# Attention and expert layer on one core: which probability chunks a DMA turns, and where the first expert's weight pieces are split

## The chip, the core and the metric

The kernel runs on one core of a Trainium2 chip. Five engines work side by side and wait for each other over semaphores: PE (TensorE, matrix products), DVE (VectorE), ACT (ScalarE), POOL (GpSimd) and SP (SyncE, which here only issues DMAs). The metric is the device time of one execution in microseconds (us), as the median of several runs.

## The reference

```python
xn = layernorm(x)                                  # x: 2 sequences x 2048 tokens x 256, float32
scores = (xn @ W_qk) @ xn.T / 16 + (kpos - qpos) * slope     # causal
s = softmax(scores) @ (xn @ W_v.T)
probs = softmax(xn @ Wr)                           # 8 experts, the best one per token
# each expert takes its first 512 tokens
ye = relu(xe @ W1[e]) @ W2[e] * p_tok              # W1: 256 x 1024, W2: 1024 x 256
out = x + s * silu(scatter(ye))
```

## The kernel before

Numbers in float32 are held as a high and a low half in float16, and each product is three matmuls (high x high, high x low, low x high). ACT writes the high half, DVE the low half, which is the number minus the high one.

The 4096 tokens are 32 tiles of 128 rows, 16 per sequence. Tile t of a sequence attends to the keys up to itself, in chunks of four blocks of 128 keys: `chunks(t)` is 1 for the first four tiles of a sequence, then 2, 3, and 4 for tiles 12 to 15 and 28 to 31. A tile goes through these steps, chunk by chunk:

- `score` on PE writes 128 x 512 scores into one of two banks of PSUM; DVE's `score` (L965) reads them, adds the bias and keeps the least value. A bank is free for the next but one chunk only then. PE works one tile ahead: in tile t it makes the scores of tile t + 1.
- `probs` on ACT takes the exponential, after the last chunk's least value (`rmin`).
- The chunk has to be turned, so that keys lie on partitions. There are two ways. PE's `turn` (L1409) makes four 128 x 128 transposes into PSUM, from which ACT (`high`, L1224) and DVE (`low`, L984) write the halves into `pT`. Or, where `by_dma(t, c)` holds, ACT and DVE write the halves of the rows into one of two buffers `p_rows`, and SP issues one transposing DMA into `pT` (`chunk_turn`, L522). ACT's `high` of such a chunk waits until the DMA of the next but one before it, in the same buffer, has landed.
- `values` on PE (L1420) multiplies the turned chunk with the values, 12 matmuls for four blocks, in tile t + 1; for a chunk turned by DMA it waits for the landing (`pT_in`). `finish` on DVE divides.

Each engine runs its own list in the order in which the program writes it: `tile(t)` goes over the steps `c`, and in each step `score(t + 1, c)`, `values(t - 1, c)` and `turn(t, c)` on PE, or `score(t + 1, c)`, `low(t, c)` and then `between(t, c)` on DVE. An instruction that waits holds up all that stands behind it on its engine. SP's list holds, besides the turns of chunks, the copies of each group of four tiles (`group_out`: two of 512 KB; `group_in` and `group_s`: one each), four transposing DMAs per group for the normed input (`turn`, xT), and the round trip by which the maximum of a weight reaches all partitions (`spread`).

The first expert's weights are prepared during attention. They are eight pieces; `FIRST_MAX` names the tiles in which DVE takes a piece's largest value, `FIRST_SCALE` the tile in which DVE makes the scale from them (`scale(0, 0)`, six small operations that wait for `spread`), and `FIRST_SPLIT` the tiles in which ACT and DVE split a piece (w_h, w_l). After tile 27 (`REST` is 28) the eight experts follow, and then tiles 28 to 31, whose scores' first part is made in the last expert. In the last expert phase a gather by POOL fetches the gate rows of these four tiles (`last_g`), and DVE scales half of them, once, at the end of tile `REST + 1`.

Of the kernel before, what the change touches and what calls it, by code (L numbers as in the profile page):

```python
# [28 lines left out]
NT = S // P  # L29
TILES = B * NT  # L30
GT = 4
GTOK = GT * P
NG = NT // GT
# [26 lines left out]
REST = TILES - GT  # L60
# [15 lines left out]
def chunks(t):  # L76

    return t % NT // GT + 1 if 0 <= t < TILES else 0


def chunk_no(t, c):
    return sum(chunks(k) for k in range(t)) + c
# [22 lines left out]
def layer_kernel(nc, x, w_qk, w_v, slope, w_r, w_e, out, slots, rows, tops, gates):  # L105


    with ExitStack() as ctx:
# [237 lines left out]
        def steps(t):  # L346
            return range(max(coming(t), chunks(t), left(t)))
# [4 lines left out]

        def by_dma(t, c):

            if t == REST - 1:
                return False
            return c in {3: (1,), 4: (1, 2)}.get(chunks(t), ())

        def turn_no(t, c):

# [2 lines left out]
        def dma_no(t, c):  # L363

            return chunk_no(t, c) - turn_no(t, c)
# [45 lines left out]

        SPLIT_TILE = {2: 3, 3: 6, 4: 10, 5: 13, 6: 15}
        STATS_TILE = {4: 3, 8: 4, 11: 5, 13: 6, 14: 7}
        FIRST_MAX, FIRST_SCALE, FIRST_SPLIT = (9, 9, 9, 9, 10, 10, 10, 11), 12, (13, 13, 13, 14, 15, 20, 21, 22)
        SECOND_MAX = (25, 25, 26, 26, 26, 27, 27, 27)
        SECOND_LOAD = 23
        FIRST_ROWS = REST - 2
# [35 lines left out]
        def parts_to(g, j):  # L453

            return {0: j + 1, 1: GT + 1 + j // 2}.get(g, GT + 1 + g)
# [12 lines left out]
        def _(sp):  # L468
# [28 lines left out]
            def group_in(g):  # L497
                k, n = g % 2, (g // 2 + 1) * 16

                sp.wait_ge(xn_made, parts_to(g, GT - 1))  # L500
                if g == 1:
                    sp.wait_ge(xn_rest, 1)
                sp.wait_ge(out_first[k], n)
                sp.wait_ge(rows_x[k], n)
                sp.dma_start(xg[k][:, :, :], x_g[g + 2]).then_inc(x_in[k], 16)

            def group_s(g):

                sp.wait_ge(s_made, g * GT + GT)
                sp.dma_start(rows_g[g][:, :, D:2 * D], so[g % 2][:, :, :]).then_inc(rows_s[g % 2], 16)  # L510
# [11 lines left out]
            def chunk_turn(t, c):  # L522

                i = dma_no(t, c)
                sp.wait_ge(pT_lo, chunk_no(t, c) + 1)
                sp.wait_ge(pv_full, t - 1)
                sp.dma_start_transpose(pT[:, t % 2, c * GT:c * GT + GT, :, :].rearrange("p b h t -> p (b h) t"),
                                       p_rows[i % 2][:, :, :, :].rearrange("p b h t -> p (b h t)")
                                       ).then_inc(pT_in[i % 2], 16)
# [11 lines left out]
            for t in range(REST):  # L541
                g = t // GT
                if t % GT == 0 and g + 1 < LATE and g + 1 != NG + 1:
                    group_out(g + 1)
                if t % GT == 1:
                    if g + 1 <= NG:
                        group_in(g + 1)
                    if g:
                        group_s(g - 1)
                if t == SPLIT_TILE[NG + 1]:  # L550
                    group_out(NG + 1)
                    group_in(NG + 1)
                for c in steps(t):
                    if by_dma(t, c):
                        chunk_turn(t, c)
                for n in (*SPLIT_TILE, LATE):
                    if t == {5: 14, LATE: REST - 8}.get(n, SPLIT_TILE.get(n)):
                        turn(n)
                if t == FIRST_SCALE - 1:
                    spread(0)  # L560
                if t == SECOND_LOAD:

                    sp.wait_ge(w_lo, 2 * PIECES)
                    sp.dma_start(raw[:, :, :], w_k[1]).then_inc(w_in[1], 16)
                if t == FIRST_ROWS:
                    for k in range(NX):
                        sp.wait_ge(slots_out[k], len(range(k, GROUPS, NX)) * GT * 16)
                    next_rows(0)
                    next_rows(1)
# [235 lines left out]
        def _(dve):  # L805
# [299 lines left out]
            def between(t, c):  # L1105

                if t in STATS_TILE:
                    norm_stats(STATS_TILE[t], part(GT, t, c))
                    if last_step(t, c):
                        norm_var(STATS_TILE[t])  # L1110
                for q in share(FIRST_MAX, t, c):
                    dve.wait_ge(w_in[1], 16)
                    largest(raw, q)
                if (t, c) == (FIRST_SCALE, 1):
                    scale(0, 0)
                for q in share(FIRST_SPLIT, t, c):
                    split_low(raw, 0, 0, q)
                for q in share(SECOND_MAX, t, c):
                    dve.wait_ge(w_in[1], 32)
                    largest(raw, q)  # L1120
# [33 lines left out]

            for t in range(REST, TILES):
                tile(t)
                if t == REST + 1:

                    dve.wait_ge(last_gates, GT * 16)
                    step(v.tensor_scalar(last_g[:, 2:GT, :], last_g[:, 2:GT, :], value_mul[:, 0:1], None, ALU.mult))  # L1160
# [451 lines left out]
```

## Time and profile before

| | us |
|---|---|
| median of 3 runs (445.28 to 446.4) | 446.22 |
| the profiled execution | 445.72 |
| its span | 444.0 |
| PE busy | 424.4 |
| DVE busy | 324.9 |
| ACT busy | 220.7 |
| POOL busy | 231.8 |

The span is the time from the first to the last instruction in the profile. Busy times of PE come from modelled ends: matmuls overlap, so the distance between two starts is what one costs, and the listed duration is longer.

### The profile page before, as it was taken

How to read it: one execution, taken by the hardware profiler on the slowest of the kernel's cores; microseconds unless marked ns; L12 is line 12 of the kernel's file. 1: busy time of each engine (PE TensorE's matmuls, PEld its weight loads, DVE VectorE, ACT ScalarE, POOL GpSimd, SP SyncE). 2: the span in 40 equal slices, each digit the busy share in tenths (PEclk: the TensorE clock that was granted, in tenths of full speed). 3: DMA queues.
4: the chain of work that ended last, by engine and by line, in shares of the span. 5: the costliest groups of instructions: out<-in, count | busy, mean ns of one | idle time of the engine just before them, and what ended most of it. 6: DMA issues, size and time to landing. Idle time of an engine off the chain costs nothing.

```text
span 444.0 us, 8419 instructions
## 1 busy us (share of the span) xinstructions
PE 424.4 (96%) x3050; PEld 290.7 (65%) x3050; DVE 324.9 (73%) x839; ACT 220.7 (50%) x436; POOL 231.8 (52%) x360
## 2 busy tenths in 40 slices
PE   5799899999899899999999999999999999999986
PEld 2377576776557677676676666666666666676765
DVE  5989768987898578778757887979796967425463
ACT  1755365344655245644434555545455545457440
POOL 5247860834726745145201657585767665848520
PEclk9999999999999999999999999999999999999999
DMA  7992856244965553255536586977877772434443
GB/s 238 356 363 73 230 124 188 60 108 100 264 161 91 115 178 56 90 215 124 121 43 245 163 263 202 224 241 180 277 183 259 163 201 71 137 107 119 112 49 95
DMA packets 92536, 73.12 MB, mean 165 GB/s; under 512 B 61519, under 2 KB 86364, under 8 KB 90448
## 3 DMA queue, kind: packets, MB, share of 16 engines
q1 hardware_dynamic: 81232, 50.22, 43.3%
q0 software_dynamic: 5824, 16.74, 12.3%
q10 hardware_dynamic: 5440, 5.64, 4.0%
q8 instruction: 24, 0.39, 0.4%
q14 instruction: 16, 0.13, 0.1%
HBM read 31.33 MB, written 28.58 MB: 135 GB/s over the span
## 4 chain that ended last, share of the span: by engine, by line
PE 68%; DVE 14%; DMA 7%; issue 4%; ACT 3%; POOL 2%; SPq 0%; another core or an unknown queue 0%; ACTq 0%; POOLq 0%; DVEq 0%
PE bank L1347 18%; PE bank L1349 18%; PE bank L1348 18%; PE bank L1436 4%; PE bank L1439 3%; PE bank L1438 3%; DVE sc L972 3%; PE bank L1417 2%; DMA pT<-p_rows 2%; DMA xg<-in_x 2%; DVE stats L820 2%; DVE pT L993 1%; ACT sc L1221 1%; DVE p_rows L993 1%; DVE w_l L1044 1%
## 5 line engine op out<-in xcount | busy, mean ns | idle before, releaser
L1436 PE MATMUL bank<-v_h,pT 128*128 128x257 f16 x272 | 74.7, 274 | 2.5 <-DMA pT<-p_rows 2.4
L1439 PE MATMUL bank<-v_h,pT 128*128 128x257 f16 x272 | 74.1, 272 | 0.0
L1438 PE MATMUL bank<-v_l,pT 128*128 128x256 f16 x272 | 73.7, 271 | 0.0
L1248 ACT ACTIVATE hid_h<-bank 128x512 f16<-128x512 f32 x64 | 38.0, 594 | 66.3 <-PE bank L1349 60.0
L1062 DVE SCALAR_TENSOR_TENSOR hid_l<-bank,hid_h 128x512 f16<-128x512 f32 x64 | 43.9, 686 | 36.5 <-ACT hid_h L1248 31.9
L1348 PE MATMUL bank<-w_l,hid_h 128*128 128x256 f16 x256 | 69.8, 273 | 0.0
L1347 PE MATMUL bank<-w_h,hid_h 128*128 128x256 f16 x256 | 69.8, 273 | 0.0
L1349 PE MATMUL bank<-w_h,hid_l 128*128 128x256 f16 x256 | 69.8, 273 | 0.0
L1237 ACT ACTIVATE pT<-bank 128x512 f16<-128x512 f32 (+3 forms) x57 | 28.8, 505 | 73.6 <-PE bank L1417 71.8
L972 DVE CUSTOM_DVE_ANT_0 sc<-bank,bias,score_mul 128x512 f32<-128x512 f32 (+2 forms) x80 | 53.0, 664 | 11.3 <-PE bank L1349 10.7
L1347 PE MATMUL bank<-xT,qT_h 128*128 128x512 f16 (+3 forms) x160 | 55.1, 347 | 4.7 <-DVE cmin L972 4.0
L1348 PE MATMUL bank<-xT,qT_h 128*128 128x512 f16 (+3 forms) x160 | 55.1, 347 | 0.0
L1349 PE MATMUL bank<-xT,qT_l 128*128 128x512 f16 (+3 forms) x160 | 55.1, 347 | 0.0
L1221 ACT ACTIVATE sc<-sc,rmin 128x512 f32<-128x512 f32 (+2 forms) x72 | 43.9, 661 | 18.0 <-DVE rmin L979 15.3
L1347 PE MATMUL bank<-xeT,w_h 128*128 128x512 f16 x128 | 48.6, 379 | 0.0
L1348 PE MATMUL bank<-xeT,w_h 128*128 128x512 f16 x128 | 48.5, 379 | 0.0
L1349 PE MATMUL bank<-xeT,w_l 128*128 128x512 f16 x128 | 48.5, 379 | 0.0
L993 DVE SCALAR_TENSOR_TENSOR pT<-bank,pT 128x512 f16<-128x512 f32 (+3 forms) x57 | 32.8, 575 | 15.4 <-ACT pT L1237 12.4
L1436 PEld LDWEIGHTS bank<-v_h,pT 128*128 128x128 f16 x272 | 26.4, 97 | 13.3 <-DMA pT<-p_rows 3.5
L1438 PEld LDWEIGHTS bank<-v_l,pT 128*128 128x128 f16 x272 | 26.8, 98 | 8.9
L668 POOL TENSOR_SCALAR xn<-xg,mv,rstd 128x256 f32<-128x256 f32 x24 | 31.0, 1296 | 3.0 <-DVE xnr L862 2.4
L1242 ACT ACTIVATE w_h<-raw,wup 128x512 f16<-128x512 f32 x40 | 27.8, 714 | 9.5 <-DVE ymul L1038 9.5
(183 smaller groups left out, 916.9 us busy)
## 6 DMA issues: line engine op xcount, KB each, us to landing
raw<-in_w_e SPq DMA_DIRECT2D x5, 2048.0 KB
sc<-in_w_e SPq DMA_DIRECT2D x3, 2048.0 KB
slots<-empty ACTq DMA_DIRECT2D x1, 4224.0 KB, 19.5
gates<-gate SPq DMA_DIRECT2D x8, 512.0 KB
out<-xg SPq DMA_DIRECT2D x7, 512.0 KB
rows<-xg SPq DMA_DIRECT2D x7, 512.0 KB
rows<-so SPq DMA_DIRECT2D x7, 512.0 KB
xg<-in_x SPq DMA_DIRECT2D x6, 512.0 KB, 4.1
```

Source lines behind the costliest of these rows:

```text
L668: last = g_.tensor_scalar(xn[:, j, :], xg[g % 2][:, j, :], mv[g % 2][:, j, 0:1], rstd[g % 2][:, j:j + 1], ALU.subtract, ALU.mult)
L972: last = v.tensor_tensor_reduce(sc[:, k, c * GTOK:c * GTOK + w], score_bank(t, n)[:, 0:w], bias[:, lo:lo + w], score_mul[:, 0:1], 3e38, AL ...
L993: v.scalar_tensor_tensor(lo, in_blocks(p), P_UP, hi, ALU.mult, ALU.subtract).then_inc(pT_lo, 1)
L1062: v.scalar_tensor_tensor(hid_l[:, f % HB, :], sc_ps[f % 2][:, :], 0.0, hid_h[:, f % HB, :], ALU.max, ALU.subtract).then_inc(h_lo, 1)
L1221: a_.activation(sc[:, k, cols], sc[:, k, cols], ACT.Exp, bias=least(t), scale=-1.0).then_inc(exp_made, 1)
L1248: a_.activation(hid_h[:, f % HB, :], sc_ps[f % 2][:, :], ACT.Relu).then_inc(h_hi, 1)
L1347: pe.matmul(ps, a_h, b_h, start=first, stop=False, skip_group_check=shared)
L1348: pe.matmul(ps, a_h, b_l, start=False, stop=False, skip_group_check=shared)
L1349: return pe.matmul(ps, a_l, b_h, start=False, stop=last, skip_group_check=shared)
L1436: pe.matmul(pv_ps[t % 2][:, 0:D + 1], p_h, v_h[:, at, q, 0:D + 1], start=kb == 0, stop=False)
L1438: pe.matmul(pv_ps[t % 2][:, 0:D], p_h, v_l[:, at, q, :], start=False, stop=False)
L1439: last = pe.matmul(pv_ps[t % 2][:, 0:D + 1], p_l, v_h[:, at, q, 0:D + 1], start=False, stop=kb == t % NT)
```

## The change

`by_dma` holds for more chunks: the first two of three in tiles 8 to 11 and 24 to 26 (before: the second), and the first three of four in tiles 12 to 14 and 28 to 30 (before: the second and third). In tile 15 it is the second alone, in tile 31 none. That is 33 chunks, before 23. On SP `group_in` of group 5 comes behind the turns of tile 13's chunks. On DVE `scale(0, 0)` stands in step 2 of tile 12 rather than step 1, and the scaling of `last_g` after tile 30 rather than tile 29. The eight splits of the first expert's weights take place in other tiles: one in tile 13 (before three), and one more in each of tiles 18 and 22.

```diff
         def by_dma(t, c):
 
-            if t == REST - 1:
+            if t in (REST - 1, TILES - 1):
                 return False
-            return c in {3: (1,), 4: (1, 2)}.get(chunks(t), ())
+            if chunks(t) == 4:
+                return c == 1 if t == NT - 1 else c in ((0, 1, 2) if t < NT else (0, 1, 2))
+            return chunks(t) == 3 and c < 2
...
-        FIRST_MAX, FIRST_SCALE, FIRST_SPLIT = (9, 9, 9, 9, 10, 10, 10, 11), 12, (13, 13, 13, 14, 15, 20, 21, 22)
+        FIRST_MAX, FIRST_SCALE, FIRST_SPLIT = (9, 9, 9, 9, 10, 10, 10, 11), 12, (13, 14, 15, 18, 20, 21, 22, 22)
...
                 if t == SPLIT_TILE[NG + 1]:
                     group_out(NG + 1)
-                    group_in(NG + 1)
                 for c in steps(t):
                     if by_dma(t, c):
                         chunk_turn(t, c)
+                if t == SPLIT_TILE[NG + 1]:
+                    group_in(NG + 1)
...
-                if (t, c) == (FIRST_SCALE, 1):
+                if (t, c) == (FIRST_SCALE, 2):
                     scale(0, 0)
...
                 tile(t)
-                if t == REST + 1:
+                if t == REST + 2:
 
                     dve.wait_ge(last_gates, GT * 16)
```

SP's list from tile 9 into tile 13, before. `pT<-p_rows` turns a chunk, `xT<-xnr` is the normed input of group 4, `tops` and `gate` are the round trip of the weight scale, `out<-xg` and `rows<-xg` are `group_out` at the beginning of tile 12:

```order
L527 DMA_TRANSPOSE pT<-p_rows 128x8x128 x2
L489 DMA_TRANSPOSE xT<-xnr 128x4x128 x4
L527 DMA_TRANSPOSE pT<-p_rows 128x8x128
L477 DMA tops<-wmax 128x2
L479 DMA gate<-tops 128x256
L494 DMA out<-xg 128x4x256
L495 DMA rows<-xg 128x4x256
L527 DMA_TRANSPOSE pT<-p_rows 128x8x128 x2
L505 DMA xg<-in_x 128x4x256
```

And after the change:

```order
L529 DMA_TRANSPOSE pT<-p_rows 128x8x128 x4
L491 DMA_TRANSPOSE xT<-xnr 128x4x128 x4
L529 DMA_TRANSPOSE pT<-p_rows 128x8x128 x2
L479 DMA tops<-wmax 128x2
L481 DMA gate<-tops 128x256
L496 DMA out<-xg 128x4x256
L497 DMA rows<-xg 128x4x256
L529 DMA_TRANSPOSE pT<-p_rows 128x8x128 x3
L507 DMA xg<-in_x 128x4x256
```

Chunk 0 of tile 11 stands behind the xT transposes, as chunk 1 did and does; chunk 0 of tile 12 stands behind the round trip and the two copies, and chunk 2 is the third of a row.

DVE in tile 12, before, from the low half of chunk 0 on. `sc,cmin<-bank` reads scores of tile 13, `pT<-bank` and `p_rows<-sc` are low halves of tile 12, and `wtop` to `ymul` is the scale:

```order
L993 SCALAR_TENSOR_TENSOR pT<-bank,pT 128x4x128
L972 ISA sc,cmin<-bank,bias,score_mul 128x512
L972 ISA cmin 128x1
L993 SCALAR_TENSOR_TENSOR p_rows<-sc,p_rows 128x4x128
L1033 TENSOR_REDUCE wtop<-gate 128x2
L879 TENSOR_SCALAR wexp<-wtop 128x2
L880 TENSOR_SCALAR wexp<-wexp 128x2
L881 TENSOR_SCALAR wup<-wexp 128x2
L883 TENSOR_SCALAR wdn<-wexp 128x2
L1038 TENSOR_SCALAR ymul<-wdn 128x1
L972 ISA sc,cmin<-bank,bias,score_mul 128x512
```

And after the change:

```order
L996 SCALAR_TENSOR_TENSOR p_rows<-sc,p_rows 128x4x128
L975 ISA sc,cmin<-bank,bias,score_mul 128x512
L975 ISA cmin 128x1
L996 SCALAR_TENSOR_TENSOR p_rows<-sc,p_rows 128x4x128
L975 ISA sc,cmin<-bank,bias,score_mul 128x512
L975 ISA cmin 128x1
L996 SCALAR_TENSOR_TENSOR p_rows<-sc,p_rows 128x4x128
L1036 TENSOR_REDUCE wtop<-gate 128x2
L882 TENSOR_SCALAR wexp<-wtop 128x2
```

The scale has moved behind the third chunk's scores and low half, and all three low halves go to row buffers.

DVE in the last tiles, before: the scaling of `last_g` (L1160) ahead of the scores that tile 30 reads for tile 31:

```order
L993 SCALAR_TENSOR_TENSOR pT<-bank,pT 128x2x128
L999 RECIPROCAL rinv<-bank 128x1
L1012 TENSOR_SCALAR so<-bank,rinv,value_mul 128x256
L1160 TENSOR_SCALAR so<-so,value_mul 128x512
L972 ISA sc,cmin<-bank,bias,score_mul 128x512
L972 ISA cmin 128x1
```

And after the change, where it is L1163:

```order
L996 SCALAR_TENSOR_TENSOR pT<-bank,pT 128x3x128
L1002 RECIPROCAL rinv<-bank 128x1
L1015 TENSOR_SCALAR so<-bank,rinv,value_mul 128x256
L1163 TENSOR_SCALAR so<-so,value_mul 128x512
L996 SCALAR_TENSOR_TENSOR pT<-bank,pT 128x4x128 x4
L1002 RECIPROCAL rinv<-bank 128x1
```

It now stands one tile later, with all scores read, ahead of the four low halves of tile 31, none of which is a row buffer's any more.

## Rows read from the trace of the kernel before

**Rows 1.** The page, part 1: busy us (share of the span) and instructions.
```profile
PE 424.4 (96%) x3050; PEld 290.7 (65%) x3050; DVE 324.9 (73%) x839; ACT 220.7 (50%) x436; POOL 231.8 (52%) x360
```

**Rows 2.** Waits of PE, whole span: us in total, times, longest.
```profile
PE bank L1347 <- DVE cmin L972: 4.0, 5, 1.3
```

**Rows 3.** Stage table: length, busy us (count) of five engines, clock, DMA share, GB/s.
```profile
68.00:100.00 32.00, 32.00 (x236) 22.31 (x235) 27.71 (x83) 14.66 (x33) 13.72 (x26) 1.00 0.44 113
...
114.00:125.00 11.00, 10.49 (x78) 7.29 (x75) 9.03 (x19) 7.38 (x13) 6.06 (x14) 1.00 0.86 266
...
420.00:432.00 12.00, 10.78 (x83) 7.86 (x82) 6.64 (x17) 4.89 (x10) 3.45 (x5) 1.00 0.43 54
```

**Rows 4.** Groups by form: count | busy us, mean ns | idle before, releaser.
```profile
L1417 PE MATMUL bank<-ident,sc 128*128 128x128 f32 x180 | 29.1, 273 | 0.5 <-DVE p_rows L993 0.4
L1237 ACT ACTIVATE pT<-bank 128x512 f16<-128x512 f32 x33 | 19.6, 594 | 23.6 <-PE bank L1417 22.7 <-issue 0.9
L1237 ACT ACTIVATE p_rows<-sc 128x512 f16<-128x512 f32 x23 | 13.8, 620 | 0.0
```

**Rows 5.** PE in order of time: start, us, instruction, count, [idle before, releaser].
```profile
101.66 0.27 PE L1436 MATMUL bank<-v_h,pT 128*128 128x257 f16 x1
...
102.98 0.60 PE L1417 MATMUL bank<-ident,sc 128*128 128x128 f32 x4
103.42 0.38 PE L1347 MATMUL bank<-xT,qT_h 128*128 128x512 f16 x1
...
150.11 0.28 PE L1436 MATMUL bank<-v_h,pT 128*128 128x257 f16 x1 [1.38 <-DMA pT<-p_rows]
...
164.91 0.38 PE L1347 MATMUL bank<-xT,qT_h 128*128 128x512 f16 x1
...
192.25 0.29 PE L1347 MATMUL bank<-wvr_h,xT 128*128 128x264 f16 x1 [0.84 <-DVE counts L942]
...
436.50 0.28 PE L1436 MATMUL bank<-v_h,pT 128*128 128x257 f16 x1 [0.89 <-DMA pT<-p_rows]
```

**Rows 6.** The chain of waits that ended last: start, us, what.
```profile
114.90 4.06 DMA xg<-in_x
...
130.20 0.65 DVE w_l L1044
...
146.88 3.18 DMA pT<-p_rows
...
426.46 4.01 DMA pT<-p_rows
...
433.17 3.28 DMA pT<-p_rows
```

**Rows 7.** SP's issues in order of time: start, us, DMA, count.
```profile
95.17 5.12 SPq L489 DMA_TRANSPOSE xT<-xnr  x4
...
108.51 0.51 SPq L495 DMA_DIRECT2D rows<-xg  x1
...
114.90 0.52 SPq L505 DMA_DIRECT2D xg<-in_x  x1
...
116.59 1.66 SPq L495 DMA_DIRECT2D rows<-xg  x1
123.97 0.37 SPq L505 DMA_DIRECT2D xg<-in_x  x1
```

**Rows 8.** DVE in order of time: start, us, instruction, count, [idle before, releaser].
```profile
110.12 0.42 DVE L1033 TENSOR_REDUCE wtop<-gate 128x2 f32<-128x256 f32 x1 [2.48 <-DMA gate<-tops]
...
112.18 0.74 DVE L972 CUSTOM_DVE_ANT_0 sc<-bank,bias,score_mul 128x512 f32<-128x512 f32 x1
...
113.45 0.48 DVE L972 CUSTOM_DVE_ANT_0 sc<-bank,bias,score_mul 128x256 f32<-128x256 f32 x1
...
119.49 0.75 DVE L820 BATCH_NORM_STATS2 stats<-xg 128x6 f32<-128x256 f32 x2 [0.81 <-DMA xg<-in_x]
...
164.06 0.74 DVE L972 CUSTOM_DVE_ANT_0 sc<-bank,bias,score_mul 128x512 f32<-128x512 f32 x1
...
421.96 0.49 DVE L1160 TENSOR_SCALAR so<-so,value_mul 128x512 f32<-128x512 f32 x1 [4.02 <-DMA so<-gates,slot_idx]
```

## The prediction, made before the changed kernel ran

> **What bounds the kernel now.** I read the page first, then the waits of PE, then PE's instructions in order of time, and last the rows of SP and DVE around the places where PE waits. The page shows PE at 96% of the span [rows 1]. PE waits little: 4.0 us in five places for DVE's reading of a score bank [rows 2], and a few times for a probability chunk that a DMA turned, as at 150.11 [rows 5]. The stage table says where: nothing in 68 to 100 us, 0.51 in 114 to 125, more after 420, at a granted clock of 1.00, the full 2.4 GHz, in all of them [rows 3]. So PE's instruction stream is the time, and an edit there counts in full as long as nothing that PE needs arrives later. DVE is the engine close behind, 27.71 of 32 us in 68 to 100 [rows 3].
>
> The profiled execution took 445.72 us for a span of 444.0, so 1.72 lie around it; it stands 0.5 below the median of the runs, 446.22. I work out a difference and apply it to the median.
>
> **Part 1: transposes leave PE.** Ten more chunks go by DMA net: +4 in tiles 8 to 11, +3 in 12 to 14, -1 in 15, +3 in 24 to 26, +3 in 28 to 30, -2 in 31. A chunk is four transposes. The listing says 273 ns for one [rows 4], but they overlap: four begin at 102.98 and the next matmul starts at 103.42, 0.44 us later [rows 5]. So PE loses 10 x 0.44 = 4.4 us of work: 2.64 in tiles 8 to 15, 1.32 in 24 to 26, 0.44 at the end. ACT and DVE have the same high and low halves to make, from SBUF rather than from PSUM: for ACT 620 against 594 ns [rows 4]; 0.026 x 10 is under 0.3 us on an engine that is half idle, taken as nothing.
>
> The Trainium skill (TensorE: Matmul & The Clock Gate, Part 4: PE-mode transpose) says about 275 ns for a transpose in a kernel's context. That would make 40 of them 11.0 us rather than 4.4. The duration in the row agrees with it, the distance between starts does not, and the sum goes by the distance.
>
> **Part 2: what a chunk by DMA needs.** From SP's issue to landing: 3.18 us, 4.01, 3.28 [rows 6]. Behind copies it is longer: the row copy issued at 116.59 let SP go on only at 123.97, 7.4 us, with 266 GB/s moved in that stretch [rows 7, 3]. Ends: 3.2 and 7.4. I take 3.2 where SP's queue shows no copy in front, and 5.7 where 1 MB was issued just before (halfway, as the copy of 108.51 had landed by 114.90, where SP waits for it [rows 7]). SP works in order and ACT has two row buffers, so two waits are new.
>
> (a) Tile 11, chunk 0. SP issues the four xT transposes from 95.17 to 100.29 and only then this tile's chunks [rows 7]; the first order fence of the change shows the same order afterwards, now with two. DVE, which releases the xT transposes, works nearly without a break in front of them, so they move up only by the 0.44 that tile 8 gives: chunk 0 is issued at about 99.9 and lands at 103.1. PE wants it at 101.66 [rows 5] less 1.76 (four chunks of 0.44), less what DVE holds it back. It gets there at about 101.1 and then waits 2.0. What tiles 8 to 11 gained is gone, and PE is 1.4 behind.
>
> (b) Tile 12. Chunk 0 is now behind the weight scale's round trip and the 1 MB of group_out: issued at about 108.6, landed at 114.3 by the 5.7. ACT's third chunk needs the row buffer of chunk 0, so DVE's low half of chunk 2, in DVE's program order before everything else, is made at 114.9 to 115.6, and the six small steps of scale(0, 0), 2.06 us (110.12 to 112.18 [rows 8]), come after it. Chunk 3's scores are read at 117.7 rather than 113.45 [rows 8]: DVE 4.2 late. Before, DVE stood 2.5 us for the scale's DMA [rows 8], so the edit that puts the scale after chunk 2 swaps that stand for a longer one. PE waits for that read with score(14, 1).
>
> (c) Tiles 13 to 15. DVE gets back two w_l splits, 2 x 0.65 [rows 6], and the 0.81 it stood before 119.49 for the group's x [rows 8] (4.06 from 114.90 [rows 6]), for x is no longer late against DVE. 4.2 - 1.3 - 0.8 = 2.1; the same buffer wait in tile 13, behind four copies, adds some tenths: 2.4 at tile 15. There chunk 2 is turned by PE again, and PE's wait for its landing, 1.38 [rows 5], goes; 2.4 - 1.4 = **+1.0 for the first sequence**. Below: -1.5, if (a) and half of (b) hide. Above: +3, if landings take 7.4.
>
> That DVE executes strictly in order is in the Trainium skill too (Perfetto Trace Analysis, Tensor Engine Instruction: "ACT/DVE/GPSIMD are strict FIFO"); it speaks against this change, and the trace agrees, as the scores of chunk 2 are read only at 112.18, behind the scale that waited for a DMA [rows 8].
>
> **Part 3: pieces moved to tiles 18 and 22.** In tile 18 DVE reads score(20, 0) at 164.06 to 164.80 and PE starts the next score in the same bank at 164.91 [rows 8, 5]: no slack. A split before it costs 0.8 (ACT's half, 0.6, comes first, and then DVE's 0.65, of which some overlaps). In tile 22 PE already waits 0.84 for DVE's counts at 192.25 [rows 5]; a split more makes it 0.65 longer. Together **+1.5**; from +0.5, if ACT's gaps take half, to +1.6.
>
> **Part 4: tiles 24 to 26.** SP's queue is empty but for the 2 MB weight load of 187.8. The chunks of step 0 are needed a full tile later, some 6 us after their low half, and a landing takes 3.2 to 5.7. **-1.3**; no less than -1.3, and 0 if the load delays them.
>
> **Part 5: the last four tiles.** The scaling of last_g waited 4.02 us on DVE for its gather [rows 8], and PE waited for the score read behind it, up to 1.3 [rows 2]. After tile 30 the gather has long landed, so this goes. PE's wait of 0.89 for the turned chunk of tile 31 [rows 5] goes as well, for PE turns it: 2 x 0.44. What is late next is the third chunk of tiles 28, 29 and 30, for the buffer. The chain of waits already has such landings near its end, at 430.47 and 436.45 [rows 6]. In tile 30: the last scores of tile 29's turn come at 421.5, chunk 0 lands at 425.4 (3.2) to 426.8 (4.6), chunk 2's low half is done at 426.7 to 428.1, then the read of score(31, 3), four-column minimum and exp: turn(31, 0) starts at 428.4 to 429.9. From there PE runs on (a full chunk of values is 1.32, from 101.66 to 102.98 [rows 5], three blocks of one 0.99): 0.44 + 1.32 + 0.44 + 1.32 + 0.44 + 0.99 + 0.44 + 4 x 1.32 = 10.7, end 439.1 to 440.6; before, it is 436.50 + 3 x 1.32 = 440.5 [rows 5]. **-0.9**; -1.4 to +1.2, the upper end if tile 30's first landing takes 5.7.
>
> **Sum:** 1.0 + 1.5 - 1.3 - 0.9 = +0.3. On the median, 446.22 + 0.3 = **446.5**: no change. (About 0.3%, 1.3 us, is what a measurement of this kernel can tell from none.) Adding the terms' ends as independent ones gives -3 to +3 and the range of this case alone is 445.0 to 447.8.
>
> **Rivals.**
> *Faster: the turns hide.* For it: PE waits nowhere in 68 to 100, and most DMA chunks land well before PE wants them. Then (a) costs nothing and (b) only what the scale cost before: first sequence -2.6 - 1.4 = -4.0, sum -4.7, 441.5. Half of that, with one of the two waits real, is -2.7. I put the case at 443.5. Against it: the rows of SP's queue.
> *Slower: the row buffers become the bound.* Place: the third chunk of tiles 12, 13 and 30. Price: a landing of 7.4 rather than 5.7 adds 1.7 in tile 12, about 1.4 in tile 13 where two megabytes are in front, and in tile 30 a landing 1.4 later adds the same to the end: +4.5, of which DVE's later gaps return 1.5. Sum +3.3, 449.5. It decides from the point at which chunk 0 lands later than DVE reaches chunk 2's low half. For it: a DMA share of 0.86 in 114 to 125 [rows 3]; against it: DVE has gaps after 150.
> *By the skill's rule on transposes*: 6.6 less than the sum, 439.9. The starts in rows 4 speak against it.
> That the change doesn't do what it says has no place here: the order fences show it.
>
> **Chances.** No change 0.37; the turns hide 0.32; buffers bound 0.30; the page's rule 0.01. The faster case is spread from 440 to 444.9 and the slower one from 447.6 to 450.5; leaving out a tenth on each side gives 442.5 to 449.8. Faster by over 0.3%: 0.33 (hide and page); within: 0.37; slower: 0.30.
>
> **What would show it.** PE's transposes: 140 for 180. In tile 12 a wait of PE for a turned chunk at about 101 to 103 (a), and DVE idle for over 4 us before the low half of chunk 2, released by ACT (b): if that idle is under 2.5, the faster case holds. PE idle at tile 19's score and at the counts of tile 23 (part 3). In the tail DVE's 4.02 gone, and ACT waiting for landings in tiles 28 to 30. The prediction is wrong in its core if tile 16 begins earlier than before.

## The result, and the profile after

The changed kernel takes 448.98 us (447.86 to 450.13, 4 runs) beside 446.09 for the kernel before on the same chip. The ratio is 1.0065, with a 95% interval of 1.0049 to 1.0081: 2.9 us slower, which is more than a measurement of this kernel needs to tell it from no change. The prediction was 446.5 (442.5 to 449.8), with "no change" as the likeliest case. The time lies in the range, but the forecast case did not happen, and the range holds it only because it made room for the rivals; the one that stood closest is "the row buffers become the bound" (449.5). (In the tables below a ratio is worked out over the runs with disturbed ones left out, so it need not be that of the two medians.)

The profiled execution took 447.86 us for a span of 446.1, 2.1 more than before. Page, part 1 (as [rows 1]), three groups (as [rows 4]: count | busy us, mean ns | idle before, releaser), the stage table for the stretches of [rows 3], and the waits of PE and of ACT (us in total, times, longest):

```profile
PE 420.9 (94%) x3010; PEld 286.3 (64%) x3010; DVE 323.0 (72%) x839; ACT 221.4 (50%) x436; POOL 230.5 (52%) x360
```

```profile
L1420 PE MATMUL bank<-ident,sc 128*128 128x128 f32 x140 | 23.1, 273 | 0.5 <-ACT sc L1224 0.5
...
L996 DVE SCALAR_TENSOR_TENSOR p_rows<-sc,p_rows 128x512 f16<-128x512 f32 x33 | 23.1, 699 | 17.5 <-ACT p_rows L1240 15.4 <-issue 2.1
...
L1240 ACT ACTIVATE p_rows<-sc 128x512 f16<-128x512 f32 x33 | 20.1, 626 | 28.3 <-DMA pT<-p_rows 28.1 <-issue 0.3
```

```profile
68.00:100.00 32.00, 31.36 (x234) 21.30 (x233) 28.13 (x87) 14.97 (x33) 13.83 (x26) 1.00 0.64 137
114.00:125.00 11.00, 7.04 (x49) 4.34 (x48) 7.87 (x22) 6.70 (x12) 5.17 (x9) 1.00 0.84 251
420.00:432.00 12.00, 11.43 (x81) 7.62 (x80) 8.20 (x22) 6.42 (x12) 4.63 (x5) 1.00 0.74 120
```

```profile
PE bank L1350 <- DVE cmin L975: 8.0, 9, 2.0
PE bank L1439 <- DMA pT<-p_rows: 4.0, 3, 1.8
```

```profile
ACT p_rows L1240 <- DMA pT<-p_rows: 28.1, 9, 10.2
```

The 40 transposes are gone. ACT's high halves of row buffers, which stood for nothing before [rows 4], now wait 28.1 us in nine places for a buffer to land; PE waits 8.0 us for DVE's score reads, before 4.0 [rows 2]. Of the three stages, that from 114 to 125 us lost most: PE is busy 7.04 of 11 us, before 10.49 [rows 3].

Where the time went is seen in the start of PE's first score matmul of a tile's first chunk, read from PE's instructions in order of time (us; the scores of tile n are made in tile n - 1):

| PE begins | before | after | difference |
|---|---|---|---|
| scores of tile 12 | 91.42 | 90.28 | -1.13 |
| scores of tile 14 | 112.98 | 112.87 | -0.12 |
| scores of tile 15 | 125.29 | 128.33 | +3.04 |
| scores of tile 16 | 137.94 | 142.37 | +4.43 |
| scores of tile 20 | 161.86 | 166.27 | +4.41 |
| scores of tile 25 | 192.94 | 198.03 | +5.09 |
| values of tile 27, the last before the experts | 225.17 | 228.70 | +3.53 |
| scores of tile 29 | 400.97 | 404.50 | +3.53 |
| last matmul | 440.37 | 442.53 | +2.16 |

All of the loss, and more, comes in tiles 13 and 14. The rows there, first the chain of waits (start, us, what):

```profile
107.17 7.84 DMA pT<-p_rows
115.10 0.64 ACT p_rows L1240
115.76 0.69 DVE p_rows L996
...
123.29 5.32 DMA pT<-p_rows
...
131.45 4.98 DMA xg<-in_x
```

SP's issues, which answer to [rows 7]:

```profile
107.17 10.54 SPq L529 DMA_TRANSPOSE pT<-p_rows  x3
...
120.63 1.40 SPq L497 DMA_DIRECT2D rows<-xg  x1
123.29 8.02 SPq L529 DMA_TRANSPOSE pT<-p_rows  x3
131.45 0.48 SPq L507 DMA_DIRECT2D xg<-in_x  x1
```

ACT's high half of tile 12's third chunk, DVE (as [rows 8]) and PE (as [rows 5]), in order of time:

```profile
115.10 0.63 ACT L1240 ACTIVATE p_rows<-sc 128x512 f16<-128x512 f32 x1 [10.17 <-DMA pT<-p_rows]
```

```profile
115.76 0.69 DVE L996 SCALAR_TENSOR_TENSOR p_rows<-sc,p_rows 128x512 f16<-128x512 f32 x1 [6.61 <-ACT p_rows L1240]
...
118.01 0.47 DVE L975 CUSTOM_DVE_ANT_0 sc<-bank,bias,score_mul 128x256 f32<-128x256 f32 x1
...
129.36 0.69 DVE L996 SCALAR_TENSOR_TENSOR p_rows<-sc,p_rows 128x512 f16<-128x512 f32 x1 [1.10 <-ACT p_rows L1240]
...
136.46 0.75 DVE L823 BATCH_NORM_STATS2 stats<-xg 128x6 f32<-128x256 f32 x2 [0.78 <-DMA xg<-in_x]
```

```profile
102.94 0.28 PE L1439 MATMUL bank<-v_h,pT 128*128 128x257 f16 x1 [1.77 <-DMA pT<-p_rows]
...
115.06 0.28 PE L1439 MATMUL bank<-v_h,pT 128*128 128x257 f16 x1 [0.73 <-DMA pT<-p_rows]
...
118.55 0.39 PE L1350 MATMUL bank<-xT,qT_h 128*128 128x512 f16 x1 [1.99 <-DVE cmin L975]
...
122.57 0.39 PE L1350 MATMUL bank<-xT,qT_h 128*128 128x512 f16 x1 [1.23 <-DVE cmin L975]
...
135.13 0.39 PE L1350 MATMUL bank<-xT,qT_h 128*128 128x512 f16 x1 [1.41 <-DVE cmin L975]
...
138.72 0.39 PE L1350 MATMUL bank<-xT,qT_h 128*128 128x512 f16 x1 [0.80 <-DVE cmin L975]
...
153.20 0.28 PE L1439 MATMUL bank<-v_h,pT 128*128 128x257 f16 x1 [1.48 <-DMA pT<-p_rows]
```

Read downwards, this is one chain. Tile 12's first chunk is issued at 107.17 and lands 7.84 us later. ACT stands 10.17 us for its row buffer, DVE 6.61 us behind ACT. The last scores of tile 13, which are ready, are read at 118.01, before at 113.45 [rows 8]. PE, with both score banks full, stands 1.99 and, a chunk later, 1.23 us. Tile 13 repeats it on a smaller scale (landing 5.32 us, DVE 1.10), and the group's x, issued at 131.45 and not at 123.97 as before [rows 7], makes DVE stand once more.

### The profile page after: what moved, and what is told of

It reads as the page before. It is cut to its first block, busy times and chain, and to the rows that moved or that the text cites. A ratio compares the mean times of both kernels' runs of the same rounds, so it can differ in the third digit from the quotient of the medians.

```text
span 446.1 us, 8359 instructions
## 1 busy us (share of the span) xinstructions
PE 420.9 (94%) x3010; PEld 286.3 (64%) x3010; DVE 323.0 (72%) x839; ACT 221.4 (50%) x436; POOL 230.5 (52%) x360
## 4 chain that ended last, share of the span: by engine, by line
PE 69%; DVE 12%; DMA 9%; ACT 5%; issue 3%; another core or an unknown queue 0%; SPq 0%; ACTq 0%; DVEq 0%
PE bank L1350 18%; PE bank L1352 18%; PE bank L1351 18%; DMA pT<-p_rows 7%; PE bank L1439 4%; PE bank L1442 4%; PE bank L1441 4%; DVE sc L975 3%; DMA xg<-in_x 2%; PE bank L1420 2%; DVE p_rows L996 2%; ACT sc L1224 2%; DVE stats L823 1%; ACT p_rows L1240 1%; DVE pT L996 1%
## 5 line engine op out<-in xcount | busy, mean ns | idle before, releaser
L1240 ACT ACTIVATE pT<-bank 128x512 f16<-128x512 f32 (+3 forms) x47 | 22.7, 485 | 44.1 <-PE bank L1420 44.0
L996 DVE SCALAR_TENSOR_TENSOR p_rows<-sc,p_rows 128x512 f16<-128x512 f32 x33 | 23.1, 699 | 17.5 <-ACT p_rows L1240 15.4
L654 POOL TENSOR_TENSOR rec<-var,power 128x4 f32<-128x4 f32 x8 | 8.3, 1041 | 50.7 <-DVE var L836 50.7
L1240 ACT ACTIVATE p_rows<-sc 128x512 f16<-128x512 f32 x33 | 20.1, 626 | 28.3 <-DMA pT<-p_rows 28.1
```

What stands on the lines that cost most here:

```text
L996: v.scalar_tensor_tensor(lo, in_blocks(p), P_UP, hi, ALU.mult, ALU.subtract).then_inc(pT_lo, 1)
L1240: a_.activation(hi, in_blocks(p), ACT.Copy, scale=P_UP).then_inc(pT_hi, 1)
```

## The experiments

Theory B, as the expectations call it, is this chain: a third chunk per tile needs the buffer of the first one, whose landing is late, and DVE stands behind it with score reads in its queue. Its rivals are PE's own waits for landings, the moved pieces, and the transfers as such. Ratios are against the kernel before on the same chip, with 95% intervals.

| kernel | median us | ratio | PE begins scores of tile 16, against before |
|---|---|---|---|
| changed kernel | 448.98 | 1.0065 (1.0049 to 1.0081) | +4.43 |
| twelve_two | 442.36 | 0.9920 (0.9904 to 0.9935) | -1.50 |
| third_buffer | 444.52 | 0.9958 (0.9945 to 0.9971) | -0.91 |
| copy_early | 448.54 | 1.0046 (1.0029 to 1.0064) | +3.26 |
| scale_step1 | 450.40 | 1.0090 (1.0072 to 1.0107) | +4.52 |
| group_in_front | 450.49 | 1.0107 (1.0093 to 1.0122) | +6.49 |
| three_alone | 454.39 | 1.0192 (1.0178 to 1.0205) | +6.20 |
| last_g_alone | 444.09 | 0.9964 (0.9951 to 0.9976) | -0.12 |
| two_fewer | 440.27 | 0.9904 (0.9869 to 0.9939) | -2.89 |
| splits_back | 440.58 | 0.9865 (0.9823 to 0.9907) | -2.19 |
| tail_none | 440.16 | 0.9854 (0.9812 to 0.9896) | -1.82 |
| tail_pairs | 439.70 | 0.9856 (0.9817 to 0.9895) | -2.71 |
| three_freed | 441.59 | 0.9901 (0.9878 to 0.9924) | -4.57 |

The last four intervals and that of two_fewer overlap; between those five kernels only the traces tell more.

### twelve_two: the second and third chunk only, in tiles 12 to 14

```diff
-                return c == 1 if t == NT - 1 else c in ((0, 1, 2) if t < NT else (0, 1, 2))
+                return c == 1 if t == NT - 1 else c in ((1, 2) if t < NT else (0, 1, 2))
```

> The changed kernel, with tiles 12 to 14 turning two chunks by DMA (the second and third) as before; all other edits stay. Theory B (the row buffer binds): ACT's high half of tile 12's third chunk waited for a buffer whose landing took 7.84 us, so DVE, in order, stood 6.61 us and read tile 13's last scores late; with two chunks per tile no third one needs a buffer early, tile 16 begins about 4 us earlier than in the changed kernel (at about 138.5, before it was 137.94), and the time is 445.0 (444.3 to 446.0). Rival L (late landings stop PE itself: its wait of 1.77 us for tile 11's first chunk and 0.73 for tile 12's): only the 0.73 goes, less 1.3 of transposes that come back, 449.5. Rival M (the moved pieces load DVE in tiles 14 to 18): 449.

Three transposed chunks given back to PE made the kernel 6.6 us faster than the changed one (442.36), 1.9 below the lowest time that theory B gave. Of this, 5.9 are there at the scores of tile 16 (+4.43 to -1.50). ACT's waits for landings fall from 28.1 us to these:

```profile
ACT p_rows L1240 <- DMA pT<-p_rows: 11.5, 4, 5.1
```

Rivals L and M, at 449.5 and 449, are out as the cause of the loss at tile 16. PE's own waits for landings do cost something beside it: that for tile 11's first chunk stays, at 1.83, and two_fewer below shows what it and one more are worth.

### third_buffer: the same three chunks, but one more buffer

```diff
+        p_rows.append(hid_h[:, 0:2, :].rearrange("p m n -> p (m n)").rearrange("p (b h t) -> p b h t", b=GT, h=2))
...
+            return (i % 3, i % 3, i // 3) if i < first else ((i - first) % 2, 3 + (i - first) % 2, (i - first) // 2)
```

> The changed kernel with a third row buffer (in memory that only the experts use otherwise) in tiles 8 to 26; the last tiles keep two. Theory B: ACT makes the high half of tile 12's third chunk at about 105.5 instead of 115.10, DVE's stand of 6.61 us goes and what is left is its wait for the scale's DMA (about 1.5), the last scores of tile 13 are read by 113 instead of 118.01 and PE's waits of 1.99 and 1.23 go: 444.5 to 446 (445.2). Rival L: PE's waits for landings stay, 448.5. Rival T (the transfers themselves are too much beside each other, since the queue is in order): the third chunk lands as late as before and PE waits for it instead, 448.5 to 449.5.

The median is 444.52 and tile 16's scores begin 5.3 us earlier than in the changed kernel. DVE around the scale of tile 12:

```profile
108.79 0.69 DVE L1002 SCALAR_TENSOR_TENSOR p_rows<-sc,p_rows 128x512 f16<-128x512 f32 x1
109.57 0.42 DVE L1042 TENSOR_REDUCE wtop<-gate 128x2 f32<-128x256 f32 x1
...
111.32 0.47 DVE L981 CUSTOM_DVE_ANT_0 sc<-bank,bias,score_mul 128x256 f32<-128x256 f32 x1
```

The stand of 6.61 us is gone altogether, and the last scores are read at 111.32 instead of 118.01, with the same transfers in flight. So it is the buffer, not the amount of traffic. Part of the rest is rival L's: PE still waits for tile 12's first chunk itself, 1.02 us at 115.07. (The median is 2.2 above twelve_two's, but the two profiled spans, 441.5 and 442.0, do not show such a difference, so what makes it is not known.)

### copy_early: the megabyte in front of tile 12's turns moved

```diff
-                if t % GT == 0 and g + 1 < LATE and g + 1 != NG + 1:
+                if t % GT == 0 and g + 1 < LATE and g + 1 not in (NG, NG + 1):
...
+                if t == 10:
+                    group_out(NG)
```

> The changed kernel with the two 512 KB copies of group 4 (out and rows) issued behind tile 10's chunk turns instead of ahead of tile 12's. Theory B with its cause (the landing is late because 1 MB was issued just in front): tile 12's first chunk is issued at about 106.2 and lands in 3.2 us, at 109.4, not 115.01; the third chunk's high half follows at once, DVE stands about 1 us rather than 6.61, and tile 16 begins about 4.5 us earlier: 444.8 (444 to 446). The copies may delay group 4's transposes (94.5 to 99.7), which tile 12 needs only at 110. Rival: the landing is long for want of buffers or because of POOL's traffic, not for the copies: it stays at 6 to 8 us, and the time at 448 to 449.

448.54, so the forecast of 444.8 failed. Three of its steps did. First, the landing took 5.75 us instead of 7.84, not 3.2: the copies are about 2 us of it, and what is left was not traced to one cause (the broadcast of the weight scale is the DMA just in front). Secondly, the copies in their new place held up tile 11's chunk: SP issued it at 100.21 instead of 99.73, PE stood 2.26 us for it instead of 1.77, and then ran for a while at the lower level of its clock, with 0.21 us between two starts instead of 0.11. PE and the stage table:

```profile
103.44 0.40 PE L1441 MATMUL bank<-v_h,pT 128*128 128x257 f16 x1 [2.26 <-DMA pT<-p_rows]
```

```profile
103.40:107.00 3.60, 3.56 (x16) 2.20 (x17) 2.12 (x9) 1.26 (x2) 2.15 (x6) 0.55 0.24 39
```

At the scores of tile 14 PE was 1.94 behind the kernel before, the changed kernel 0.12 ahead. This part of the loss has nothing to do with the row buffers. It does not save the forecast: the four runs with a mean granted clock of 1.000 took 447.5 to 447.8 us. Thirdly, the stand moved on. ACT in order of time:

```profile
112.73 0.63 ACT L1242 ACTIVATE p_rows<-sc 128x512 f16<-128x512 f32 x1 [7.35 <-DMA pT<-p_rows]
...
127.95 0.63 ACT L1242 ACTIVATE p_rows<-sc 128x512 f16<-128x512 f32 x1 [5.91 <-DMA pT<-p_rows]
```

At the scores of tile 15 PE was only 0.46 behind the kernel before (changed kernel: 3.04), but one tile later ACT waited 5.91 for tile 13's buffer instead of 4.08, because tile 13's first turn, behind the copies of group 5, took 7.15 us: it was issued 2.57 us earlier than in the changed kernel and landed only 0.74 earlier (127.87, not 128.61). 2.8 of the loss came back, and PE stood another 1.03 us at 228.75 for the experts' rows (`xeT`). The Trainium skill (DMA: Bandwidth & Descriptors, Queues, rings and completion order) says that on each DMA engine descriptors are consumed in ring order; the trace agrees as far as landings behind copies take 5.0 to 8.1 us in these runs (4.97 in three_alone, 8.12 in group_in_front) and mostly 3.0 to 3.3 where no copy stands in front; that the 5.75 here had none just in front shows that ring order is not all of it.

### scale_step1: the scale ahead of the stand

```diff
-                if (t, c) == (FIRST_SCALE, 2):
+                if (t, c) == (FIRST_SCALE, 1):
```

> The changed kernel with the first scale (six small DVE operations) back in step 1 of tile 12, ahead of the third chunk's low half. Theory B: its 1.6 us run inside DVE's stand of 6.61 us, the last scores of tile 13 are read at 116.4 instead of 118.01, PE's wait of 1.99 falls to 0.4: -1.5, 447.5. Rival (the scale waits for its own DMA for longer than the buffer is late): no change or slower, 449 to 450.

```profile
109.48 0.42 DVE L1036 TENSOR_REDUCE wtop<-gate 128x2 f32<-128x256 f32 x1 [2.48 <-DMA gate<-tops]
...
115.63 0.69 DVE L996 SCALAR_TENSOR_TENSOR p_rows<-sc,p_rows 128x512 f16<-128x512 f32 x1 [3.42 <-ACT p_rows L1240]
116.24 0.48 DVE L975 CUSTOM_DVE_ANT_0 sc<-bank,bias,score_mul 128x256 f32<-128x256 f32 x1
...
129.58 0.69 DVE L996 SCALAR_TENSOR_TENSOR p_rows<-sc,p_rows 128x512 f16<-128x512 f32 x1 [2.78 <-ACT p_rows L1240]
```

The read at 116.24 (forecast 116.4) and PE's wait there (0.36, forecast 0.4) came as worked out, and the scores of tile 15 began 1.46 us earlier than in the changed kernel. The time did not: DVE, earlier in tile 13, stood 2.78 us for that tile's buffer instead of 1.10, and at tile 16's scores the gain was gone (+4.52): tile 13's first turn was issued 1.76 us earlier than in the changed kernel (121.53) but landed 0.22 later (128.83). Why it landed no earlier was not tested. The median, 450.4, is 1.4 over the changed kernel's; its trace shows an extra wait of 1.3 us of PE for the experts' rows (`xeT`), whose cause was not tested. As in copy_early, a gain ahead of the next buffer wait was worth nothing.

### group_in_front: the load of group 7 back ahead of tile 13's turns

```diff
                     group_out(NG + 1)
+                    group_in(NG + 1)
```

(and not behind the turns.)

> The changed kernel with the load of group 7's rows back ahead of tile 13's chunk turns on SP. Theory B: that load is issued at about 124 instead of 131.45 and DVE's wait of 0.78 for it at 136.46 goes, but the three turns of tile 13 are issued behind it, the first at about 124.5 instead of 123.29, and with 0.5 MB more in front; ACT's third high half of tile 13, which waited 4.08 us, waits 1 to 2 us longer: +0.5, 449.5 (448.5 to 451). Rival X (the late load is what costs tile 14 and 15 their 1.4 us): 447.6.

SP, DVE and PE, each in order of time:

```profile
126.79 0.37 SPq L507 DMA_DIRECT2D xg<-in_x  x1
127.27 17.28 SPq L529 DMA_TRANSPOSE pT<-p_rows  x6
```

```profile
132.29 0.69 DVE L995 SCALAR_TENSOR_TENSOR p_rows<-sc,p_rows 128x512 f16<-128x512 f32 x1 [4.16 <-ACT p_rows L1239]
```

```profile
131.59 0.28 PE L1438 MATMUL bank<-v_h,pT 128*128 128x257 f16 x1 [1.93 <-DMA pT<-p_rows]
```

450.49, slower by 1.5 than the changed kernel. SP stands for the group's copies to land before it may issue the load, and the turn comes at 127.27 instead of 123.29. DVE stands 4.16 instead of 1.10, but what PE loses is already there before that: PE itself stands 1.93 for the landing of tile 13's first chunk, for which it does not wait in the changed kernel. Against the changed kernel it is 1.97 late at the values of tile 13 and 2.06 at the scores of tile 16. So this edit of the change helped, by some 2 us at tile 16, because it takes a wait out of SP's queue in front of the turns. Rival X is out.

### three_alone: the third chunk put into the kernel before

```diff
+            if 12 <= t < 15:
+                return c < 3
             return c in {3: (1,), 4: (1, 2)}.get(chunks(t), ())
```

> The kernel before with one edit alone: tiles 12 to 14 turn their first chunk by DMA as well. Theory B (the third chunk waits for a row buffer, here with the copies of tiles 12 and 13 in front): PE saves 3 x 0.44 of transposes, and what the first sequence lost against two chunks per tile (4.43 + 1.50 = 5.9 us at tile 16) comes nearly whole, less what only the late x and the later scale added: +3 to +5, 450.3 (449.3 to 451.3). Rival (the loss came from the edits around it: the scale behind chunk 2, the group's load behind the turns): 445 to 446.5.

454.39: slower by 8.5, beyond both cases. At the scores of tile 16 PE is +6.20, so three chunks in tiles 12 to 14 alone cause a loss larger than the whole change's, and the edits around them are not needed for it. It is not DVE's stand alone: at 130.64 PE itself stood 2.37 for the landing of tile 13's first chunk, which SP issued behind the group's load, as in group_in_front. 1.5 more came during the experts, from what was not looked into. The rest is the tail, DVE and PE in order of time and two stretches of the stage table (columns as in [rows 3]):

```profile
432.88 0.49 DVE L1162 TENSOR_SCALAR so<-so,value_mul 128x512 f32<-128x512 f32 x1 [7.55 <-DMA so<-gates,slot_idx]
```

```profile
434.21 0.61 PE L1349 MATMUL bank<-xT,qT_h 128*128 128x512 f16 x1 [4.75 <-DVE cmin L974]
```

```profile
434.00:436.50 2.50, 2.29 (x6) 0.89 (x7) 2.03 (x6) 0.00 (x0) 0.72 (x1) 0.50 0.00 0
438.00:442.00 4.00, 4.00 (x32) 2.92 (x30) 2.03 (x7) 1.31 (x3) 0.00 (x0) 1.00 0.50 92
```

The wait for the last gather grew from 4.02 [rows 8] to 7.55 us, PE stood 4.75, and then ran at a granted clock of 0.50, 1.2 GHz. The profiled execution is 3.5 above its median, so its tail is that of a longer execution than most; tile 16 is not touched by that.

### last_g_alone: only the scaling of the gathered rows moved

```diff
-                if t == REST + 1:
+                if t == REST + 2:
```

> The kernel before with DVE's scaling of the last group's gathered rows one tile later, and nothing else. If DVE's wait of 4.02 us for the gather is what delays tile 31's third score (PE's 1.22 at 423.30, and 1.03 more of DVE after it), PE reaches the end about 1.2 us earlier, with the wait for tile 31's turned chunk (0.89) left or up to 0.5 larger: -0.8, 445.4 (444.8 to 446.2). Rival: the landing of tile 31's chunk at 436.45 sets the end and does not move: within 0.3, 446.2.

```profile
421.37 0.38 PE L1347 MATMUL bank<-xT,qT_h 128*128 128x512 f16 x1
```

```profile
428.12 0.48 DVE L1160 TENSOR_SCALAR so<-so,value_mul 128x512 f32<-128x512 f32 x1
```

444.09, 1.8 faster, more than the forecast's 0.8 and below its range. DVE no longer waits for the gather, and tile 31's third score starts at 421.37 with no wait, before at 423.30. From the scores of tile 29 to the last matmul PE gained 1.39, in the changed kernel 1.37. So in this pair the whole gain of the tail is this one edit, and tail_pairs, which has the chunks of the kernel before there and the moved scaling, gained 1.34.

### two_fewer: two more chunks back to PE

```diff
-            if t in (REST - 1, TILES - 1):
+            if t in (NT - 1, REST - 1, TILES - 1):
...
-                return c == 1 if t == NT - 1 else c in ((1, 2) if t < NT else (0, 1, 2))
-            return chunks(t) == 3 and c < 2
+                return c in ((1, 2) if t < NT else (0, 1, 2))
+            return chunks(t) == 3 and c < 2 and (t, c) != (11, 0)
```

> The kernel that turns two chunks by DMA in tiles 12 to 14 (442.36 us), with two more chunks given back to PE: the first of tile 11 and the second of tile 15. PE waited 1.83 us for the one's landing at 103.00 (it stands behind four xT transposes) and 1.45 for the other's at 146.95; each costs PE 0.44 of transposes. If these waits are PE's own and nothing is late behind them: -1.4 and -1.0, 440.0 (439.5 to 441.0). Rival (DVE, whose score reads come right behind, holds PE by the same amount): 441.5 to 442.5.

440.27 as worked out (440.0). Both waits are gone. Beside twelve_two, PE is 2.5 us ahead at the scores of tile 14, 1.0 at those of tile 17 and 2.6 at those of tile 18, past tile 15's chunk, against 2.4 in the forecast.

### splits_back: the first expert's pieces in their old tiles

```diff
-        FIRST_MAX, FIRST_SCALE, FIRST_SPLIT = (9, 9, 9, 9, 10, 10, 10, 11), 12, (13, 14, 15, 18, 20, 21, 22, 22)
+        FIRST_MAX, FIRST_SCALE, FIRST_SPLIT = (9, 9, 9, 9, 10, 10, 10, 11), 12, (13, 13, 13, 14, 15, 20, 21, 22)
```

> The fastest kernel so far (440.27 us: two chunks by DMA in tiles 12 to 14, one in tile 11, none in tile 15) with the first expert's pieces split in the tiles of the kernel before (13, 13, 13, 14, 15, 20, 21, 22). The prediction priced the moved pieces at +1.5, so back again they should bring -1.5 from tile 18 on, 438.8. In the traces tiles 18 to 24 cost 0 to 1.1 us more than before, and tile 13 gets two splits (1.4 us of DVE) where DVE has waits of 1.28 and less: 440.3 (439.8 to 441.0), no change; slower, 441 to 441.7, if tile 13's DVE work is PE's time.

440.58, no change from 440.27 (the ratios, 0.9865 and 0.9904, have intervals that overlap). The old places cost 0.7 by tile 16's scores (-2.19 instead of -2.89). The new ones cost between the scores of tiles 20 and 25 0.7 in the changed kernel, 1.1 in third_buffer and nothing in two_fewer. The +1.5 of the prediction is not there. (The profiled execution is 4.4 above the median; only its part up to the experts is read. In its tail PE stood 2.07 us and then ran at a granted clock of 0.60 over 3.7 us.)

### tail_none and tail_pairs: the last four tiles

tail_none (tail_pairs has the first line as well, and keeps `NT - 1`):

```diff
-            if t in (NT - 1, REST - 1, TILES - 1):
+            if t in (NT - 1, REST - 1):
...
-                return c in ((1, 2) if t < NT else (0, 1, 2))
+                return c in (1, 2)
```

> The fastest kernel so far with two chunks by DMA (second and third) in tiles 28 to 30 and none in tile 31. Theory B in the tail: DVE's read of tile 31's last scores stands behind tile 30's third low half, whose high half waited 3.3 us for a row buffer; PE's 1.20 before tile 31's first turn and 0.49 at tile 30 go, 3 x 0.44 of transposes come back: -0.4, 439.9 (439.4 to 440.4). Rival (the third chunk hides and saves its transposes): +1.3, 441.6.

> The fastest kernel so far with the last four tiles as in the kernel before: the second and third chunk by DMA in tiles 28 to 31. Against the kernel with none in tile 31 PE loses 0.88 of transposes and waits about 0.9 for the landing of tile 31's second chunk: within 0.3 of it, 439.9 (439.3 to 440.5). If it is so, all of the tail's gain over the kernel before is the moved scaling of the gathered rows.

440.16 and 439.70 beside 440.27: all within 0.6. Three chunks by DMA in tiles 28 to 30, two, or two with tile 31's as well are worth the same. In two_fewer PE stands 1.20 us before tile 31's first turn, in tail_none for nothing there, and pays 1.32 in transposes instead. tail_pairs has the lowest median of the study, 6.2 us under the kernel before.

### three_freed: three chunks with both obstacles out of the way

third_buffer's buffers and copy_early's move on top of tail_pairs, with

```diff
+                return c < 3 and (t < NT or c > 0)
```

> The fastest kernel so far (439.7 us: two chunks by DMA in tiles 12 to 14, the second in tile 11, none in tile 15, the last tiles as before) with three by DMA in tiles 12 to 14, a third row buffer up to tile 26, and group 4's copies issued behind tile 10's turns. It takes both causes out of the way of the third chunk: no buffer wait, and less in front of tile 12's first landing. If the turns then hide, the three transposes groups saved count: -1.3, 438.4. If each landing only waits elsewhere (tile 13's first chunk landed 7.15 us after its issue with group 4's copies moved, and PE stood 0.71 for it; with a third buffer alone PE stood 1.02 for tile 12's): 439.7 to 441.0.

The median is 441.59, not the 438.4 of a gain, and 0.6 above the rival's range; whether it is slower than tail_pairs the two intervals, which overlap, leave open. The trace says that the turns do hide up to tile 16 once they may: at the scores of tile 16 PE is 4.57 ahead of the kernel before, in tail_pairs 2.71, so 1.86 gained (1.3 of transposes expected). 1.1 of it is gone by tile 27 (-5.39 and -4.65), nearly all in one wait of PE for the experts' rows (`xeT`, 1.00 at 218.49), and the rest and more in the last ten microseconds. PE and the stage table:

```profile
430.93 0.28 PE L1447 MATMUL bank<-v_h,pT 128*128 128x257 f16 x1 [2.10 <-DMA pT<-p_rows]
```

```profile
424.00:428.90 4.90, 4.83 (x44) 4.06 (x42) 2.62 (x5) 2.68 (x5) 1.06 (x2) 1.00 0.55 30
428.90:430.90 2.00, 0.00 (x0) 0.00 (x0) 0.95 (x3) 0.00 (x0) 0.00 (x0) 1.00 0.72 151
431.80:436.00 4.20, 4.20 (x25) 3.09 (x24) 0.00 (x0) 0.00 (x0) 0.00 (x0) 0.59 0.18 59
```

A turned chunk of tile 31 landed late, PE stood 2.10 us, and then ran at half clock for most of the next five microseconds. What makes that landing late in this kernel was not tested.

## Why the prediction was right or wrong

**Part 1, right.** 140 transposes for 180. Tiles 8 to 10 give 1.13 by the scores of tile 12 (three chunks of 0.44 less what DVE held, the fourth counts later).

**Part 2 (a), right.** PE waited 1.77 at 102.94 for tile 11's first chunk (forecast: 2.0, landing at 103.1), and values began 1.28 behind (forecast 1.4). two_fewer shows that the chunk is not worth turning by DMA.

**Part 2 (b), the mechanism right, the time in part by luck.** Forecast: issue 108.6, landing 114.3, DVE's low half 114.9 to 115.6, last scores read at 117.7. Measured: 107.17, 115.01, 115.76 to 116.45, 118.01. The landing took 2.1 us longer than the 5.7, and the issue came 1.4 earlier than worked out; that the two misses cancel is luck. DVE was 4.56 late, forecast 4.2.

**Part 2 (c), wrong: this is the term that was mis-sized, +1.0 for a measured +4.4.** The prediction let DVE win back 1.3 from the moved pieces and 0.8 from the x of group 7, "for x is no longer late against DVE", and put the same wait in tile 13 at "some tenths". Measured is +4.43 at the scores of tile 16, where PE's tile 15 begins, not 2.4. The load of x had itself been moved behind turns that wait for DVE, and came at 131.45, so DVE stood 0.78 for it. And what DVE regained ahead of a buffer wait was lost in it in scale_step1 and in copy_early, where the next landing came hardly earlier (0.22 later and 0.74 earlier than in the changed kernel) although its issue did by 1.8 and 2.6 us: such a landing is a wall, not a debt that later gaps pay. Last, PE's 1.38 at tile 15's turned chunk did not go: with one chunk by DMA left there, PE stood 1.48 for that one (153.20). 2.0 too little late, 1.4 counted as gained: 3.4 together.

**Part 3, too high:** about +0.7 for +1.5. The prediction took the end of a read at 164.80 and the next matmul at 164.91 [rows 8, 5] as "no slack" and charged 0.8 for it; the scores of tile 21 begin 0.32 later against those of tile 20 than before, with a wait of PE for DVE of 0.15 in the row. (That read, of tile 20's first scores, is made in tile 19 and not in tile 18; the split of tile 18 stands right ahead of it, so the place was right.) Those of tile 25, behind the counts, lose 0.47 for a forecast of 0.65.

**Part 4, right:** -1.56 from tile 25's scores to the end of attention in tile 27 (forecast -1.3), so these three chunks do hide. 0.26 of it is there in last_g_alone too, which has no such chunk, so they give 1.3.

**Part 5, right in sum.** -1.37 for -0.9. PE starts turn(31, 0) at 431.91, which is 428.6 when the 3.3 that the tail began late are taken off, and runs on from there, as worked out (428.4 to 429.9). What the forecast did not part is which edit gives it: last_g_alone and tail_pairs, with the chunks of the kernel before, gain 1.39 and 1.34, so the moved scaling alone is enough. It is not safe either: with the changed kernel's tail twelve_two and two_fewer gained nothing there (last section).

The sum of the measured terms is 4.4 + 0.7 - 1.6 - 1.4 = +2.1, the difference of the two profiled spans. The first sequence is off by 3.4 and the other three terms by 1.6 the other way, so the forecast time was nearer than its largest term. **The rivals:** "row buffers become the bound" is the mechanism, shown by twelve_two and third_buffer, though for another price than it named: the landing of 7.84 is there in tile 12, but the larger part is that the later gaps returned nothing, for which it had taken off 1.5. Its third place, tile 30, cost nothing that these medians can tell (440.27 with three chunks there, 440.16 with two). "The turns hide" held for tiles 8 to 10 and 24 to 26, and in three_freed for tiles 12 to 14. By the figure for a transpose of the Trainium skill (TensorE: Matmul & The Clock Gate, Part 4: PE-mode transpose), about 275 ns, the 12 of three chunks would give an estimated 3.3 us; tiles 8 to 10 gave 1.13 and three_freed 1.86. So the rival at 439.9 is out. (Its evidence, the starts, stands in [rows 5] and not in rows 4.)

## What to carry to other kernels

Before an engine's work is handed to a DMA, count the buffers that it goes through against the landing time at that place of the queue: with two buffers and a landing of 8 us the third piece stops its writers, and all that stands behind them in order. What the engine regains ahead of the next such wait may be lost in it, as in scale_step1, so gaps downstream must not be subtracted from the price without a look at that landing. Price each edit at its own wait, and test it alone: here one edit alone gained 1.8 us, another alone lost 8.5, a third gave some 2 back, and the sum hid all of them. When an experiment goes another way than forecast, look at the granted clock too: in copy_early a part of the loss was PE at half clock.

## What the runs showed that was not expected

- A stand of PE can cost beyond its length. The granted clock fell after stands of 2.07 us (splits_back, to 0.60 over 3.7 us), 2.10 (three_freed, 0.59 over 4.2), 2.26 (copy_early, 0.55 over 3.6) and 4.75 (three_alone, 0.50 over 2.5): the lower of the two levels for most or all of the stretch. The length of the stand does not tell it alone: two of 2.37 and 2.35 us in tile 14 of three_alone left the clock at 1.00, as did those of 1.1 to 2.0 us after the first 95 us in the traces of before and after.
- A transpose of one chunk from SBUF to SBUF landed in 3.0 to 3.3 us at best, 4.0 to 5.8 with other traffic, and with about a megabyte of copies issued just ahead in 5.0 (three_alone), 5.3 and 7.8 (both in the changed kernel) and up to 8.1 (group_in_front). What sets the place in this range stays open.
- Landings in the last tiles varied from kernel to kernel by more than the edits there: the same tail code gave -1.37 in the changed kernel, +0.55 in twelve_two and +0.10 in two_fewer, against the kernel before. Why stays open.
